# First dense attention: order of the maxima products, POOL and ACT for the maxima's row, seven banks for the last two pairs

## The reference

```
qkv = x @ qkv_w + qkv_b
q, k, v = to_heads(split(qkv))          # (B, 16, 1024, 8)
q, k = apply_rotary(q), apply_rotary(k)
scores = einsum('bhqd,bhkd->bhqk', q, k) * SCALE
weights = softmax(scores, axis=-1)
attn = einsum('bhqk,bhkd->bhqd', weights, v)
return attn @ out_w + out_b
```

## Time and profile before

| | |
|---|---|
| median of 3 runs | 4306.52 us (4299.02 to 4309.17) |
| span of the profiled execution | 4150.6 us |
| median less span (start and end of an execution) | 155.9 us |
| PE, DVE, ACT, POOL busy in the whole span | 84%, 65%, 63%, 33% |
| first dense attention, by first and last rows | about 335 to 1168 us |

### The profile page before, as it was taken

The page is one execution under the profiler, slowest core; times in us unless marked ns, Lnnn a source line. Parts: engine busy times, 40 slices in busy tenths (PEclk is TensorE's granted clock), DMA queues, the critical chain, the costliest instruction groups (busy, mean ns, idle before and its releaser), DMA issues. The chain is left out here.

```text
span 4150.6 us, 54356 instructions
## 1 busy us (share of the span) xinstructions
PE 3473.8 (84%) x20444; PEld 1530.9 (37%) x20444; DVE 2690.9 (65%) x4473; ACT 2596.3 (63%) x4281; POOL 1360.0 (33%) x1266
## 2 busy tenths in 40 slices
PE   7995888889958898988888799879987899686776
PEld 4672122212221221222222366546655456332333
DVE  5225989989746656565555677557756523568887
ACT  2221676767858989989999587548754332325554
POOL 0501482010011000010000588358840261406886
PEclk9996999999979989999999899989988999897877
DMA  4111131111021001011000111111102012290001
GB/s 141 39 42 45 38 61 29 22 32 17 2 55 26 16 20 27 7 25 16 16 1 1 28 34 35 25 23 34 35 15 86 12 56 56 49 112 6 1 16 26
DMA packets 140860, 137.40 MB, mean 33 GB/s; under 512 B 42632, under 2 KB 105908, under 8 KB 140596
## 3 DMA queue, kind: packets, MB, share of 16 engines
q1 hardware_dynamic: 131060, 116.08, 12.7%
q0 software_dynamic: 8192, 16.79, 1.8%
q10 hardware_dynamic: 1344, 1.05, 0.1%
HBM read 64.12 MB, written 33.82 MB: 24 GB/s over the span
## 5 line engine op out<-in xcount | busy, mean ns | idle before, releaser
L476 PE MATMUL PS<-t 50*128 50x512 bf16 (+2 forms) x3072 | 737.5, 396 | 203.4 <-ACT t L629 55.3
L609 ACT ACTIVATE t<-PS 128x512 f32<-128x512 f32 x1024 | 532.7, 602 | 236.2 <-PE PS L476 235.5
L748 DVE TENSOR_TENSOR t<-t 128x1536 f32<-128x1536 f32 (+1 forms) x384 | 585.1, 1591 | 122.7 <-ACT t L629 70.0
L664 DVE TENSOR_REDUCE t<-PS 128x1 f32<-128x1024 f32 x512 | 600.9, 1215 | 50.7 <-PE PS L468 46.5
L550 PE MATMUL PS<-t 128*9 128x512 f32 x4096 | 550.2, 610 | 12.7 <-DVE t L748 12.3
L476 PEld LDWEIGHTS PS<-t 50*128 50x128 bf16 (+2 forms) x3072 | 158.3, 94 | 985.2 <-ACT t L629 276.9
L631 ACT ACTIVATE t<-PS 128x1536 f32<-128x1536 f32 (+1 forms) x384 | 477.9, 1310 | 54.0 <-PE PS L476 37.1
L629 ACT ACTIVATE t<-PS 128x1536 f32<-128x1536 f32 (+1 forms) x384 | 477.1, 1310 | 34.6 <-PE PS L476 19.4
L468 PE MATMUL PS<-t 48*128 48x512 bf16 x1024 | 342.1, 404 | 45.2 <-DVE t L664 24.7
L1845 POOL TENSOR_TENSOR t<-t 128x512 f32<-128x512 f32 x128 | 159.8, 1270 | 575.8 <-ACT t L1710 575.3
L524 PE MATMUL PS<-t 128*128 128x384 f32 x544 | 269.1, 579 | 0.0
(11 more groups left out here) (413 smaller groups left out, 6329.5 us busy)
## 6 DMA issues: line engine op xcount, KB each, us to landing
t<-scr SPq DMA_DIRECT2D x336, 64.0 KB
t<-t SPq DMA_DIRECT2D x128, 128.0 KB, 2.3
scr<-t SPq DMA_DIRECT2D x96, 128.0 KB, 1.8
t<-t SPq DMA_DIRECT2D x16, 512.0 KB, 13.0
scr<-t SPq DMA_DIRECT2D x2, 2560.0 KB
t<-scr SPq DMA_DIRECT2D x16, 320.0 KB, 3.7
scr<-t SPq DMA_DIRECT2D x16, 320.0 KB, 2.6
t<-scr SPq DMA_DIRECT2D x48, 48.0 KB
```

Of the source, the lines that this page charges most:

```text
L476: return e.op.matmul(PS[:, bk, :], Kx[p // 4 % 2][lo:lo + rows, j, kb * 128:kb * 128 + 128], Qx[p // 4 % 2][lo:lo + rows, j, hf * 512:hf * ...
L609: e.op.activation(P[x % 4][:, 2 * hf + side, :], PS[:, bank((what, p, k, side, hf)), :], ACT.Exp, scale=S8).then_inc(*PW.up((p, k, side, hf)))
L664: e.op.tensor_reduce(MX[p % 2][:, side, qc:qc + 1], PS[:, 2 * side:2 * side + 2, :].rearrange("p a n -> p (a n)"), AX, ALU.max).then_inc(* ...
L748: e.op.tensor_tensor(o, o, SGM[(12 * p + 3 * blk + ti) % 3][:, 0:nu, :], ALU.mult).then_inc(*DG.up((p, blk, ti)))
```

## The change

- The prologue's maxima products of a block run side by side instead of half by half: both halves of side 0, then both of side 1.
- "parts" moves from DVE to POOL, in the order list's place; the first six gathers, which stood ahead of it on no condition, now stand behind the parts of pair 2.
- The copy of the sent row moves from DVE to ACT, and "send" stands behind k = 2 instead of k = 1.
- The copy of "turn" moves from DVE to ACT in this attention.
- From pair 30 on, the ring has seven banks (4, 5, 7, 0, 1, 2, 3), and so have the turns and projections at the end.

```
@@ order @@
-                                if k == 1 and 2 <= p + 1 < NP:
+                                if k == 2 and 2 <= p + 1 < NP:
                                     yield "send", p + 1
@@ pe @@
-                    ends = Ring(4, 5) if first else Ring(0, 3)
+                    wide = Ring(4, 5, MISC, 0, 1, 2, 3)
+                    ends = wide if first else Ring(0, 3)
...
-                            for hf in range(2):
-                                for side in range(2):
+                            for side in range(2):
+                                for hf in range(2):
                                     maxima(p, qc, side, hf)
...
-                            bm = take(e, ring.next(), ("send", p), (DV, ("mrow", p)))
-                            e.wait_ge(DV, ("parts", p))
+                            bm = take(e, ring.next(), ("send", p), (AC, ("mrow", p)))
+                            e.wait_ge(PO, ("parts", p))
...
                             rows_in(e, p)
+                            if mate(p) is None:
+                                ring = wide
...
-                            bm = take(e, (ends if b == NB - 1 else ring).next(), ("turn", b, j), (DV, ("turn", b, j)))
+                            bm = take(e, (ends if b == NB - 1 else ring).next(), ("turn", b, j),
+                                      (AC if first else DV, ("turn", b, j)))
...
-                            e.wait_ge(DV, ("turn", b, j))
+                            e.wait_ge(AC if first else DV, ("turn", b, j))
@@ act @@
+                        elif what == "send":
+                            p, = i
+                            e.wait_ge(PM, ("send", p))
+                            if p:
+                                e.wait_ge(MOUT, p - 1)
+                            e.op.copy(mrow[:], PS[0:32, bank((what, *i)), 0:128]).then_inc(*AC.up(("mrow", p)))
+                        elif what == "turn" and first:
...
+                            e.op.copy(ATT_T[j][:], PS[:, bank((what, *i)), :]).then_inc(*AC.up(("turn", b, j)))
@@ dve, and the same four operations in pool @@
-                        elif what == "parts":
...
-                        elif what == "send":
...
-                        elif what == "turn":
+                        elif what == "turn" and not first:
@@ pool @@
+                        elif what == "parts":
+                            p, = i
+                            for side in range(2):
+                                e.wait_ge(DV, ("max", p, 7, side))
+                            e.op.tensor_scalar(M[:], MX[p % 2][:], -1.0, None, ALU.mult).then_inc(*PO.up(("neg", p)))
+                            if p:
+                                e.wait_ge(PM, ("send", p - 1))
+                            then().tensor_copy(ML[:], M[:]).then_inc(*PO.up())
+                            then().tensor_copy(MP[:, :, 0, :], ML[:]).then_inc(*PO.up())
+                            e.op.tensor_tensor(MP[:, :, 1, :], M[:], ML[:], ALU.subtract).then_inc(
+                                *PO.up(("parts", p)))
```

More of the change, by code:

```diff
@@ L638, in act @@
                             e.op.copy(OS[:], PS[:, PVB, :]).then_inc(*AC.up(("os", p)))
+                        elif what == "send":
[5 more added lines that the diff above has]
+                        elif what == "turn" and first:
+                            b, j = i
+                            e.wait_ge(PM, ("turn", b, j))
+                            if b:
+                                e.wait_ge(PM, ("proj", b - 1, j))
+                            e.op.copy(ATT_T[j][:], PS[:, bank((what, *i)), :]).then_inc(*AC.up(("turn", b, j)))
                 def dve(e):
@@ L662, in maxima @@
                         if p > 1:
-                            e.wait_ge(DV, ("neg", p - 2))
+                            e.wait_ge(PO, ("neg", p - 2))
                         e.op.tensor_reduce(MX[p % 2][:, side, qc:qc + 1],
@@ L726, in dve @@
                                     maxima(mate(p), k, 1 - side)
-                        elif what == "parts":
-                            p, = i
-                            then().tensor_scalar(M[:], MX[p % 2][:], -1.0, None, ALU.mult).then_inc(
-                                *DV.up(("neg", p)))
-                            if p:
-                                e.wait_ge(PM, ("send", p - 1))
-                            then().tensor_copy(ML[:], M[:]).then_inc(*DV.up())
-                            then().tensor_copy(MP[:, :, 0, :], ML[:]).then_inc(*DV.up())
-                            e.op.tensor_tensor(MP[:, :, 1, :], M[:], ML[:], ALU.subtract).then_inc(
-                                *DV.up(("parts", p)))
-                        elif what == "send":
-                            p, = i
-                            e.wait_ge(PM, ("send", p))
-                            if p:
-                                e.wait_ge(MOUT, p - 1)
-                            e.op.tensor_copy(mrow[:], PS[0:32, bank((what, *i)), 0:128]).then_inc(*DV.up(("mrow", p)))
                         elif what == "tile" and i[1]:
@@ L883, in sp @@
                             p, = i
-                            e.wait_ge(DV, ("mrow", p))
+                            e.wait_ge(AC, ("mrow", p))
                             e.op.dma_start(mD[p].rearrange("s a (q t) -> (s a q) t", q=8), mrow[:]).then_inc(
```

## The result

| | before | after |
|---|---|---|
| median, us | 4299.02 (4293.68 to 4309.17, 5 runs) | 4276.98 (4267.43 to 4283.57, 5 runs) |
| ratio to before | | 0.9939 (95% interval 0.9923 to 0.9956) |
| span of the profiled execution, us | 4150.6 | 4279.9 |
| the same execution's own time, us | not listed | 4281.82 |
| from the attention's first maxima product to the end of its last projection's product, us | 794.2 | 767.1 |

The changed kernel is 0.6% faster: 22 us between the medians, 26 us by the ratio. The forecast was 26.6 us, and 4280, counted from 4306.52, the median of three runs of before; from the median of five, 4299.02, the same 26.6 gives 4272.4.

A forecast was written before the change was run, and what follows sets the result against it. Plain steps were taken as a PE and ACT loop over three banks, not DVE-bound. Terms -9.1 + 2.7 - 2.2 - 7.4 - 3.2 - 7.4 = -26.6 us gave 4280 us, range 4268 to 4296; forecast's chance 0.58.

The forecast's parts named there:

- Prologue, -10.1 + 1.0 = -9.1: Prologue: products by sides cut a block from 3.07 to 2.34 us (-10.1); parts on POOL add 1.0.
- Rival 3: Prologue: products of one side do not overlap, a block takes 3.49 us, prologue grows by 5.9, time 4296; chance 0.05.
- POOL's queue, +2.7 on the fetch: Before pair 5: two parts (pairs 3 and 4) in POOL's queue delay SP's fetch by 2.7 us (1.5 to 5).
- The wait at pair 5, near 11: Start of pair 5: PE's wait for its row from DRAM grows from 8.88 to near 11 us.
- rival 2: Pair 5: the wait for the row shrinks; if half goes, -31 to -35 us, time 4272; chance 0.11.
- stall for POOL in pair 3 or 4: Pairs 3 and 4: a PE stall for POOL there would be swallowed by the wait at pair 5.
- Send on ACT, -2.2 or 0.10 in a plain pair: Some 22 pairs behind pair 5: moving the sent row's copy off DVE saves 0.10 each, -2.2 us (-4 to +2).
- Where DVE was behind, -7.4: Turns, pairs 11 and 19, send waits and smaller ones: PE's waits for DVE go, -7.4 us together (-3 to -9).
- clock, -3.2: Pairs 11 and 19: the granted clock no longer falls behind waits, 1.6 us each, -3.2 (0 to -3.2).
- Seven banks, -7.4: Pairs 30 and 31: steps limited by ACT alone take 1.95 us, -7.3, and 0.1 at the end (0 to -8).
- Rivals 1, 4, 5, 6: 1: POOL's queue eats prologue, 4284, 0.13; 4: last pairs held, 0.05; 5: clock falls, 4320, 0.03; 6: last pairs only, 0.05.
- The 155.9 us around the span: Whole kernel: 155.9 us, as in the median of the runs, added to the forecast span of 4124.0, giving 4279.9.

The follow-up runs named there:

- sides alone: The kernel before with only the prologue's maxima products run side by side; 4290.97 against 4296.34 us (10 and 25 runs), ratio 0.9987.
- experiment with the gathers first: The changed kernel with the fetch behind the send and the first six gathers back ahead of the prologue; 4109.89 against 4162.74 us for before, one run each.
- the second profile: The changed kernel, unaltered, profiled again on another chip; 4271.55 us against 4303.78 for before there, ratio 0.9929.
- the ACT copies alone: The kernel before with the sent row's and turn's copies on ACT and send behind k = 2; 4146.68 against 4162.74 us, one run each, ratio 0.9961.
- seven banks alone: The kernel before with only the seven banks for pairs 30 and 31 and the turns and projections at the end; ratio 0.9982 to before.

## Why the prediction came out right, and where it did not

- **Prologue, -10.1 + 1.0 = -9.1: right.** It came out at 9.03, by the mechanism named: sides alone gave 9.95, and the two parts on POOL took 0.92 of it back. The block is 2.35 against the 2.34 forecast. The four operations took 0.98 where the slope of the earlier trace rows gave 1.2 (and DVE's own, 395.95 to 396.62 before, 0.67 and not 0.75). The prediction also worked out 1.4 from the Trainium skill ("GPSIMD Engine Reference", 4.1 Engine selection), but misapplied it: the Trainium skill gives the factor of two for operations with two inputs and has those with one roughly at line rate, and of these four only the subtraction has two. An estimate by it is 0.17 + 0.17 + 0.17 + 0.34 = 0.85 us. Rival 3 is out. The Trainium skill's account of row groups ("TensorE: Matmul & The Clock Gate", Part 3, Packing small matmuls) speaks of PE's time, and PE's time does not decide here: its four products of a block span 2.16 us in the new order (sides alone), inside DVE's 2.35.
- **POOL's queue, +2.7 on the fetch: mis-sized by half.** Counted from t0 the fetch starts 3.2 us early (153.1 to 149.9), not 6.4, so the term cost 5.8 and not 2.7, outside its bounds of 1.5 to 5. The step that failed is the sentence that the six gathers fit before 463. In time they fit; but with them there PE and DVE stand in step (1,3), which takes 3.5 us more, and the first split comes later for it. The experiment with the gathers first gave 3.3 us of it back. Of the rest 1.0 went in pair 0, and 1.3 in POOL's queue between the first split and the fetch (61.2 us before, 62.5 after).
- **The wait at pair 5, near 11: wrong.** It was gone in the first profile of after, and below the 8.88 of before in the second. The step that failed is "lets PE go 22 us after the fetch starts", taken as fixed from one sample. It was 17.6 in after and 20.7 in the second profile. The trace of before itself had 19.6 and 20.8 for the same way at pairs 13 and 21. That is rival 2's mechanism; against the fetch's 3.2 too late it more than cancels: pair 5 starts 7.6 early where 6.4 was forecast, and 4.6 in the second profile. That the first came so near is luck. PE also waited 2.6 and 2.0 for the parts in pairs 3 and 4, the "stall for POOL in pair 3 or 4" that the prediction held possible and free.
- **Send on ACT, -2.2 or 0.10 in a plain pair: the sign is right, the reason is wrong.** Steps (p,1) and (p,2) together went from 5.32 to 5.16 in after, or 3.5 us in 22 pairs, but the ACT copies alone leave them at 5.35. The 0.16 come from the parts on POOL, which the prediction had counted for nothing in a plain pair: on DVE the reductions behind them hold up PE's maxima product, and (p,2) takes 2.78 instead of 2.59.
- **Where DVE was behind, -7.4, and clock, -3.2; with the send -12.8: 12.5 measured** from pair 5 to pair 30 (11.3 in the second profile). The members differ, and the sum holds (12,7) and (20,7), which the prediction left as they are and which took 2.4 more here, by what looks like chance. The turn's wait of 1.13 was worth 0.6 in each of (8,7), (16,7) and (24,7), which went from 4.60 to 4.00: a wait taken away is not a step shortened by as much. (9,1) and (9,2) gave 0.2 and 0.55, where 0.5 was taken. (11,2) and (19,2) gave 2.8 and 2.9, forecast 2.75 each with the clock. The clock's part is shown only as far as this: with the parts and all reductions on DVE such a step took 4.74 to 4.91 in five cases, with the clock at 1.00, and 6.06 to 6.35 in the five in which it fell to 0.50, so the fall costs some 1.4; with the parts on POOL it took 3.43 to 3.45 in all ten, at 1.00. So of the 5.7 gained here some 2.8 is the clock's, by estimate, and beside an execution of before without falls, such as seven banks alone had, it would be gone.
- **Seven banks, -7.4: right**, 7.1 in after and 7.0 alone. ACT has no gap, where the earlier trace rows have 0.37 in a step, and a step takes 2.01 (seven banks alone), not the 1.95 forecast.
- **Rivals 1, 4, 5, 6.** 1 came half true (the fetch is only 3.2 early) and was undone by 2. 4 is out by the last pairs, 6 by pairs 5 to 30. 5 is out: the clock is 0.99 in the main stretch, 0.98 before.
- **The 155.9 us around the span: wrong.** Around a span lie 1.9 us (4281.82 less 4279.9). The rest fits the stalls outside the attention, which the profiled execution of before did not have; that its timed runs had them is inferred from their times. It did no harm only because the same stalls hit both kernels; on the chip without them, where before took 4162.74, the same 4280 would have been off by some 140.

The sum was so right to 0.6 us (27.2 against 26.6 from t0 on) in the first profile and 3.6 too high in the second (23.0), with two errors of 3 to 5 us at pair 5 that cancel in the first. The prologue and the last pairs held by their mechanisms; the members between pairs 5 and 30 held only as a sum.

## What to carry to other kernels

A busy share of 93% did not bound the step; the way to see the bound is to write the loop of one bank out, from the product that fills it to the reader that frees it, and count banks. A small DMA that others wait for goes ahead of a batch of large ones on its queue: that move alone was worth 14.7 us in the traces, more than half of what the whole change gave. A time that depends on a DMA queue (here 17.6 to 23.7 us from the start of the fetch to the next pair's first product, at three places in three profiles) is a range and not a number, so read it at every place where the trace has it.

## What the runs showed of the hardware that I had not expected

- The same program, before, costs 4162.74 us on one chip (one run) and 4296 to 4304 on others. The difference lies in pauses that the profile puts down to "issue": in the stretch from 108 to 178 us mostly of 3.4 to 3.6 us, and one of 11.8. PE stands while POOL goes on issuing one indirect DMA every 1.26 us. POOL issues them at the same pace in the profile of before, which has no such pause. The pause in (1,3), 3.5 us behind six of POOL's indirect DMAs, is of the same size. Both kernels that show it ran on chips with the other pauses, and no kernel with gathers in that place ran on the chip without, so that they have one cause is a guess and not shown.
- POOL's operations on 128x16 elements take 0.20 to 0.27 us, DVE's 0.17 when nothing disturbs them. The Trainium skill ("GPSIMD Engine Reference", 4.1 Engine selection) has GPSIMD at about twice VectorE's time for operations with two inputs and roughly at line rate for one. Here the one with two inputs, the subtraction, took 0.22 to 0.23 against 0.17, so less than twice; the four together took 0.98 against 0.67.
- Between the issue of a row's write to DRAM and that of its read pass 1.4 us with the fetch behind them (588.56 to 589.92). Right behind the 24 DMAs of a fetch it was 6.4 in pair 4 of after, and 5.4 to 14.2 behind its later fetches.
